# Scores by 64 rows, wider joins, and rows moved from GpSimd to ScalarE in a fused attention, FFN and scan kernel

## The reference, cut to what matters

```
x = x + attention(norm(x))      # 16 heads of 8; key k for query q if
                                #   k<=q and (k>q-32  or  (q-k)%64==0)
x = x + ffn(norm(x))            # 128 -> 512 -> 512 -> 128, weights of +1 and -1, relu
y = norm(x)
x = x + (y + scan_block(y))     # see below
x = x + ffn(norm(x))            # the same weights again

scan_block(y):                  # in the reference _mamba_block, x is y
  u, z  = split(norm(y)*g + b @ W_in)       # 2 x 256 channels
  u     = silu(causal_conv4(u))
  dt_lo, B, C = split(u @ W_xp)             # 8, 16, 16
  dt    = softplus(dt_lo @ W_dt + b_dt)     # 256 channels
  h[t]  = exp(dt*A) * h[t-1] + dt*u*B       # 256 channels x 16 states
  return res_scale * ((sum_n h*C + u*D) * silu(z)) @ W_out
```

## Time and profile before

| | |
|---|---|
| median of 3 runs | 811.17 us (809.6 to 815.29) |
| the profiled execution | 811.52 us |
| its span, first to last instruction | 809.7 us |
| mean granted TensorE clock | 0.989 of full speed |
| PE busy | 721.4 us (89%) |
| DVE busy | 695.3 us (86%) |
| POOL busy | 664.2 us (82%) |
| ACT busy | 594.8 us (73%) |
| DMA queue, 153.5 MB | 71.4% of 16 engines' span |

### The profile page before, as it was taken

One profiled execution on the slowest core, in us unless ns is written; L12 is line 12 of the kernel. 1 busy time (PEld: TensorE's weight loads), 2 busy tenths in 40 slices (PEclk: granted clock), 3 DMA queues, 4 the chain that ended last, 5 costly groups with the idle time before them and its releaser, 6 DMA issues. The chain is left out here.

```text
span 809.7 us, 22189 instructions
## 1 busy us (share of the span) xinstructions
PE 721.4 (89%) x7840; PEld 430.6 (53%) x7840; DVE 695.3 (86%) x1187; ACT 594.8 (73%) x1161; POOL 664.2 (82%) x824
## 2 busy tenths in 40 slices
PE   5999988998789999998999999899896889897887
PEld 3765655644455447545555456355452356453566
DVE  6977229999999989999889999999998989799983
ACT  5776698797788989887689978868667744764533
POOL 5143437998899989989999799899998999999961
PEclk9999999999999999999999999999999999998999
DMA  5000019888799668877777889889797899898950
GB/s 200 3 3 2 2 54 269 226 231 229 206 225 237 159 173 238 230 177 200 198 213 197 225 233 243 232 230 244 207 253 199 252 259 240 215 266 235 264 158 27
DMA packets 84177, 154.94 MB, mean 191 GB/s; under 512 B 9433, under 2 KB 10082, under 8 KB 84066
## 3 DMA queue, kind: packets, MB, share of 16 engines
q1 hardware_dynamic: 84066, 153.51, 71.4%
HBM read 142.46 MB, written 11.01 MB: 190 GB/s over the span
## 5 line engine op out<-in xcount | busy, mean ns | idle before, releaser
L1779 POOL TENSOR_TENSOR d<-d,cr 128x1024 f32<-128x1024 f32 x128 | 300.0, 2354 | 13.8 <-DVE d L1279 4.1
L1578 ACT ACTIVATE ps<-dt,An 128x512 f32<-128x512 f32 x256 | 173.7, 690 | 71.9 <-DVE d L1279 60.5
L1279 DVE TENSOR_TENSOR_SCAN d<-ps,hl,d 128x512 f32<-128x512 f32 x128 | 157.0, 1262 | 3.7 <-ACT ps L1578 3.3
L1279 DVE TENSOR_TENSOR_SCAN d<-ps,d 128x512 f32<-128x512 f32 x128 | 149.6, 1202 | 7.2 <-ACT ps L1578 6.5
L1267 DVE TENSOR_TENSOR d<-ps,d 128x512 f32<-128x512 f32 x184 | 118.5, 671 | 7.1 <-DMA d<-dud 7.1
L891 PE MATMUL ps<-h,w 128*128 128x512 f16 (+1 forms) x512 | 114.3, 373 | 3.5 <-DVE h L1224 2.8
L1766 POOL TENSOR_TENSOR d<-d,br 128x512 f32<-128x512 f32 x72 | 91.5, 1277 | 4.3 <-DMA d<-dud 4.3
L891 PEld LDWEIGHTS ps<-h,w 128*128 128x128 f16 x512 | 46.8, 98 | 70.9 <-DVE h L1224 12.8
L966 PE MATMUL ps<-d,cst 128*32 128x512 f32 x512 | 69.3, 614 | 10.6 <-POOL d L1779 6.4
L1434 ACT COPY pt<-ps 128x512 f32<-128x512 f32 x96 | 53.8, 589 | 13.9 <-PE ps L825 10.6
L825 PE MATMUL ps<-cst,sx 128*128 128x128 f32 x384 | 56.3, 281 | 8.0 <-ACT sx L1427 3.5
(11 more groups left out here) (182 smaller groups left out, 1457.1 us busy)
## 6 DMA issues: line engine op xcount, KB each, us to landing
dt<-dtd SPq DMA_DIRECT2D x256, 256.0 KB, 5.3
d<-dud SPq DMA_DIRECT2D x256, 256.0 KB, 4.8
dtd<-sR SPq DMA_DIRECT2D x16, 256.0 KB, 4.4
dud<-sE SPq DMA_DIRECT2D x16, 256.0 KB, 3.8
X<-in_x SPq DMA_DIRECT2D x8, 256.0 KB, 6.3
br<-bcd SPq DMA_DIRECT2D x8, 256.0 KB
cr<-bcd SPq DMA_DIRECT2D x8, 256.0 KB
out<-X SPq DMA_DIRECT2D x3, 512.0 KB, 5.8
```

The costliest lines, as they stand in the source:

```text
L1279: eng.tensor_tensor_scan(d, banks[u % NG][:, :], d, hl[:, r:r + 1] if m % 2 else 0.0, ALU.mult, ALU.add).then_inc(v_sc, 1)
L1578: eng.activation(banks[u % NG][:, :], DT[:, u % NT, :], ACT.Exp, scale=An[:, g:g + 1]).then_inc(s_da, 1)
L1779: eng.tensor_tensor(d, d, CR[m % 2][:, :].unsqueeze(1).to_broadcast((128, n, 512)), ALU.mult).then_inc(p_cm, n)
```

## The change

1. **Scores by 64 rows.** A unit, far or near, now holds half of the heads: 8 windows x 8 heads for far, 4 windows x 8 heads for near. `KD` has two blocks of heads per 64 partitions in place of four; a factor `rmask` blanks the other 32 partitions. Every unit pair has its masks and products on the two halves of TensorE's rows.
2. **Joins.** Two a batch instead of four, each for 512 rows and all heads; one `FR` and one `JW` in place of two.
3. **Rows by ScalarE.** Apart from one half of batch 0's attention and the first two FFN passes (`SHARED`), ScalarE normalises all rows, and a new step `mxu_s` updates X. `mno_s` takes over the two waits that `mln_p` had.
4. **Places.** All due times are new, and so is `WARM`: 33 places with 176 products, 26 of them before the first scan, instead of 28 with 152. The FFN order and the split of the drives stay.

```diff
-UNITS = [(kind, g, kk) for kind, g in GROUPS for kk in range(2 if kind else 4)]
-def near(u):
-    return (u - 8) % 4 // 2, u % 2
+UNITS = [(kind, g, kk, c) for kind, g in GROUPS for kk in range(1 if kind else 2) for c in range(2)]
...
+SHARED = FFN_ORDER[:2]
+def shared_to(i):
+    return min(i, len(SHARED))
...
-JOINS = [(b, g) for b in range(NB) for g in range(4)]
+JOINS = [(b, h) for b in range(NB) for h in range(2)]
...
-        KD = sb("KD", [128, 4, PAD + T])
+        KD = sb("KD", [128, 2, PAD + T])
...
-        ZN = [sb(f"zn{i}", [128, 8, 4, 9]) for i in range(2)]
-        MN = [sb(f"mn{i}", [128, 8, 4]) for i in range(2)]
+        ZF = [sb(f"zf{i}", [128, 8, 2, 16]) for i in range(3)]
+        ZN = [sb(f"zn{i}", [128, 16, 4, 9]) for i in range(2)]
+        MN = [sb(f"mn{i}", [128, 16, 4]) for i in range(2)]
         FC = sb("fc", [128, 2, T])
-        FR = [sb(f"fr{i}", [128, 2, 8, 2, 16]) for i in range(2)]
-        JW = [sb(f"jw{i}", [128, 4, 32]) for i in range(2)]
-        JT = sb("jt", [128, 256])
+        FR = sb("fr", [128, 16, 4, 16])
+        JW = sb("jw", [128, 4, 64])
+        JT = sb("jt", [128, 512])
...
-            def scores(b, u, mk):
-                U = NU * b + u
-                bank = bank_of["sc", b, u] = turn((s_exp, U + 1) if u in SHIFTED_T else (v_sub, shifted(b, u, "v") + 1))
-                eng.matmul(bank[:, :], e4[:, :], mk, start=True, stop=False, skip_group_check=True)
-                return bank
             def asc_t(b, u):
-                kind, g, kk = UNITS[u]
+                kind, g, kk, _ = UNITS[u]
                 U, gi = NU * b + u, group_of(u)
+                nw = 8 if kind else 4
                 if U == 0:
                     eng.wait_ge(v_set, V_SEL)
-                if kind:
-                    bank = scores(b, u, masks[:, 256:288].unsqueeze(1).to_broadcast((128, 16, 32)))
-                else:
-                    kk, _ = near(u)
-                    if g == kk == 0:
-                        mk = masks[:, 0:256].unsqueeze(1).to_broadcast((128, 2, 256))
+                half = [slice(64 * c, 64 * c + 64) for c in range(2)]
+                two = []
+                for c in range(2):
+                    by = (s_exp, U + c + 1) if u + c in SHIFTED_T else (v_sub, shifted(b, u + c, "v") + 1)
+                    bank = bank_of["sc", b, u + c] = turn(by)
+                    if kind:
+                        mk = masks[half[c], 256:288].unsqueeze(1).to_broadcast((64, 16, 32))
+                    elif g == kk == 0:
+                        mk = masks[half[c], 0:256].unsqueeze(1).to_broadcast((64, 2, 256))
                     else:
-                        mk = masks[:, 64:192].unsqueeze(1).to_broadcast((128, 4, 128))
-                    two = [scores(b, u + c, mk) for c in range(2)]
+                        mk = masks[half[c], 64:192].unsqueeze(1).to_broadcast((64, 4, 128))
+                    eng.matmul(bank[:, :], e4[half[c], :], mk, start=True, stop=False, skip_group_check=True)
+                    two.append(bank[:, :].rearrange("p (a w k) -> p a w k", a=2, w=nw))
                 if b == 0:
                     eng.wait_ge(v_aqm, gi + 1)
                 else:
                 eng.wait_ge(s_aqk, 4 * b + 2)
                 if U == 0:
                     eng.wait_ge(v_akd, 2)
+                if b == 0 and u == 8:
+                    eng.wait_ge(p_set, 2)
+                if kind == 0 and g == 2:
+                    eng.wait_ge(p_kp, b + 1)
                 qm = QM[gi % 2]
-                if kind:
-                    bw = bank[:, :].rearrange("p (a w k) -> p a w k", a=4, w=4)
-                    Ks = KD[:, :, PAD:PAD + T].rearrange("p a (h x) -> p a h x", x=128)
-                    for k in range(4):
-                        m = 8 * g + 4 * kk + k
-                        lq = qm[:, 4 * kk + k, :, :].rearrange("p a n -> p (a n)")
-                        t = eng.matmul(bw[:, :, k, :].rearrange("p a (h x) -> p a h x", x=4), lq, Ks[:, :, :, 4 * m:4 * m + 4], start=False,
-                                       stop=(k == 3 and u not in SHIFTED_T), skip_group_check=True)
-                    t.then_inc(t_sc, 1)
-                    return
-                if g == 2:
-                    eng.wait_ge(p_kp, b + 1)
-                for k in range(4):
-                    m = 8 * g + 4 * kk + k
-                    at = 64 * (m % 16) + m // 16
+                Ks = KD[:, :, PAD:PAD + T].rearrange("p a (h x) -> p a h x", x=128)
+                for k in range(nw):
+                    wi = nw * kk + k
+                    m = 8 * g + wi
                     for c in range(2):
-                        r = slice(64 * c, 64 * c + 64)
-                        for j in range(2):
-                            o = slice(64 * j, 64 * j + 64)
-                            lq = qm[r, 4 * kk + k, 2 * j:2 * j + 2, :].rearrange("p a n -> p (a n)")
-                            dst = two[c][o, :].rearrange("p (a w k) -> p a w k", a=2, w=4)[:, :, k, :]
-                            t = eng.matmul(dst, lq, KD[r, 2 * c:2 * c + 2, at:at + 127:2], start=False,
-                                           stop=(k == 3 and u + c not in SHIFTED_T), skip_group_check=True)
-                        if k == 3:
+                        end = k == nw - 1 and u + c not in SHIFTED_T
+                        if kind:
+                            for j in half:
+                                lq = qm[half[c], wi, j.start // 32:j.stop // 32, :].rearrange("p a n -> p (a n)")
+                                t = eng.matmul(two[c][j, :, k, :].rearrange("p a (h x) -> p a h x", x=4), lq, Ks[half[c], :, :, 4 * m:4 * m + 4],
+                                               start=False, stop=end, skip_group_check=True)
+                        else:
+                            at = 64 * (m % 16) + m // 16
+                            lq = qm[half[c], wi, :, :].rearrange("p a n -> p (a n)")
+                            t = eng.matmul(two[c][:, :, k, :], lq, KD[half[c], :, at:at + 127:2], start=False, stop=end, skip_group_check=True)
+                        if k == nw - 1:
                             t.then_inc(t_sc, 1)
...
             def akd_v(b, h):
                 if h == 0:
-                    eng.wait_ge(p_set, 3)
                     eng.wait_ge(t_aqk, 1)
-                    for a in range(4):
-                        t = eng.tensor_copy(KD[32 * a:32 * a + 32, a, PAD:PAD + T:2], bank_of["aqk", b, 0, 1][32 * a:32 * a + 32, :])
+                    for a in range(2):
+                        t = eng.tensor_scalar(KD[:, a, PAD:PAD + T:2], bank_of["aqk", b, 0, 1][:, :], rmask[:, a:a + 1], None, ALU.mult)
...
-            def aback_v(b, g):
-                J = 4 * b + g
-                if J >= 2:
-                    eng.wait_ge(p_jw, 5 * (J - 1))
+                eng.transpose(FC[:, c, 256 * g:256 * g + 256].rearrange("p (w q) -> p w q", w=8),
+                              ZF[(8 * b + u) % 3][:, :, :, :].rearrange("p w a n -> p w (a n)")).then_inc(v_far, 1)
+            def aback_v(b, h):
+                J = 2 * b + h
+                if J:
+                    eng.wait_ge(p_jw, 4 * J)
                 eng.wait_ge(v_far, 8 * b + 8)
-                far = FC[:, :, :].rearrange("p c (m h x i) -> p c i h m x", h=8, x=2, i=2)
+                far = FC[:, :, :].rearrange("p c (o m k x i) -> p c i k o m x", o=2, k=8, x=2, i=2)
                 for c in range(2):
-                    eng.transpose(FR[g % 2][:, c, :, :, :].rearrange("p (j o) a n -> p j (o a n)", o=2).rearrange("p j (m x) -> p j m x", x=2),
-                                  far[:, c, g // 2, 4 * (g % 2):4 * (g % 2) + 4, :, :]).then_inc(v_back, 1)
-            def jrec_v(b, g):
-                J = 4 * b + g
+                    eng.transpose(FR[:, :, 2 * c:2 * c + 2, :].rearrange("p (j o) a n -> p j o (a n)", o=2).rearrange("p j o (m x) -> p j o m x", x=2),
+                                  far[:, c, h, :, :, :, :]).then_inc(v_back, 1)
...
-            def jmix_p(b, g):
-                J = 4 * b + g
-                fr, zn, _, jw = parts(g)
+            def jmix_p(b, h):
+                J = 2 * b + h
+                fr, zn, _, jw = parts(h)
                 eng.wait_ge(v_jr, J + 1)
-                for i in (1, 0):
-                    eng.tensor_tensor(jw[i], jw[i], jw[2], ALU.mult).then_inc(p_jw, 1)
+                eng.tensor_tensor(JW[:, 0:2, :], JW[:, 0:2, :], jw[2].unsqueeze(1).to_broadcast((128, 2, 64)), ALU.mult).then_inc(p_jw, 1)
+                eng.wait_ge(p_jw, 4 * J + 1)
                 for i, x in ((1, zn), (0, fr)):
-                    eng.wait_ge(p_jw, 5 * J + 2 - i)
-                    for c in range(2):
-                        t = eng.tensor_tensor(x[:, c, :, :, 0:8], x[:, c, :, :, 0:8], jw[i][:, c, :, :].unsqueeze(3).to_broadcast((128, 8, 2, 8)), ALU.mult)
-                    t.then_inc(p_jw, 1)
-                eng.wait_ge(p_jw, 5 * J + 4)
-                for c in range(2):
```

(59 more changed lines are left out.)

397 lines of the change are left out of this document (194 added, 203 removed), and 320 rows, old and new, of tables (PLACES, WARM).

## The result

| | before | after |
|---|---|---|
| median of the runs (4 each) | 810.5 us (809.6 to 815.29) | 799.91 us (798.72 to 800.94) |
| ratio, 95% interval | | 0.9845 [0.9805, 0.9885] |
| the profiled execution, its span | 811.52, 809.7 | 800.71, 798.9 |
| mean granted clock | 0.989 | 0.981 |

On a second chip the kernel after took 799.2 us against 814.5, a ratio of 0.9794 [0.9739, 0.9849]: faster by 1.5 to 2%.

What follows compares the result with a forecast made beforehand. VectorE and GpSimd, both 93% busy between the scans, were taken as the bound. Span 809.7 - 1 + (3 - 3 - 3 - 8) + 1.5 = 799.2, so 801 us timed; range 788 to 820, the forecast's own 793 to 805.

Steps and rivals of the forecast that it cites:

- VectorE's idle time: Between first and last scan: a sign of the forecast, to fall from 47.5 us to under 40.
- GpSimd's relief, -8: Between the scans: less GpSimd work shortens VectorE's waits, 5 us for drive loads and 3 for direct waits.
- ScalarE's blocks, +3: Between the scans: 31 longer ScalarE row blocks can delay decays; 3 taken at about 1 us, ends 0 and +31.
- rival C: Between scans: ScalarE's four-row blocks hold up the decays, making the kernel slower, 818 to 824 us; chance 0.14.
- VectorE's work, -3: Between the scans: half as many, twice as wide transposes and additions save VectorE 3 us (-8 to +1).
- TensorE's scores, -3: Between the scans: cheaper score pairs save TensorE 10 us in three batches and halve VectorE's 5.4 us of score waits.
- the 1.7 that I set as the mark: TensorE's far pair: under 1.7 us would show the forecast right, over 2.5 the rival of failed packing.
- the term of 3 us that the rule would have added: TensorE's scores: if changing the tiling mode drains the array, the sum would be about 3 us higher.
- Ahead of the first scan, -1: Before the first scan: cheaper scores against a bigger join, ScalarE's rows and 26 fillers, 1 us saved (+3 to -4).
- The tail, +1.5: After the last scan: rows in sequence on ScalarE and a third layer moved there cost 1.5 us (0.5 to 4).
- My mark for the last stretch: Last 64 loads with their scans: taking longer than 62 us would show the forecast wrong.

Runs made afterwards that it cites:

- rows_only: Kernel before, in its old order, with only the rows and the X update moved to ScalarE alone: 831.16 us, ratio 1.0188.
- rows_shared: Kernel after with the rows shared by halves with GpSimd again and the X update by GpSimd: 816.62 us, ratio 1.0013.
- pool_ballast: Kernel after with unneeded 128 x 128 tiles written by GpSimd where rows and X update stood before: 807.3 us, ratio 0.9897.
- xu_split: Kernel after with ScalarE's X update cut into four one-row steps between decays: 800.76 us, ratio 0.9838.
- pe_ballast2: Kernel after with filler products on TensorE ahead of both masks of a pair, three far and one near: 829.3 us, ratio 1.0155.
- after_again: Kernel after, unchanged, timed once more as the standard for runs beside it: 799.2 us.
- The ballasts: Kernel after with unneeded work added on one engine: GpSimd 807.3 us, ScalarE 811.62, VectorE 806.58, TensorE 841.19 and 829.3.
- no_fill_head: Kernel after without the 26 filler products ahead of the first scan: 823.09 us, ratio 1.0112.

## Why the prediction was right, and where its steps were not

The time was forecast at 801 and came at 799.9, the span at 799.2 and came at 798.9. That the span hit within 0.3 us is luck. By VectorE's work and waits the terms missed by +4.1 (scores), +1.1 (ahead of the first scan), -1.3 (decays), -1.7 (tail) and -0.6 (work), 1.8 us of small waits that no term had went away besides, and these cancel. Beside the second chip's 814.5 the gain is 15 us, not 11. VectorE's idle time, which was to be under 40 us, is 40.4. Step by step:

- **GpSimd's relief, -8: the size came, the way to it is not what I wrote.** VectorE's wait for loads was to go from 7.1 to 2.1 us and went to 1.9. Busy time between the scans was forecast at 564 and is 555, a join at 6.3 us and is 6.0 (36.1 in six). The strided 512-column form takes 1.07 to 1.20 us, so the plain form's 1.28 was the right neighbour. (One of the ten instructions has 128 columns, as in my sum, not two, as in my text.) The other 3 us were to come from direct waits for GpSimd, and these gave nothing: softplus fell from 2.7 to 2.0 and the join's two from 1.9 to 0.3, but the scans now wait 2.5 for GpSimd's drives. What made up for it was ScalarE's Exp, 7.5 to 4.4, where I expected nothing. Nor do the runs bear out that GpSimd's relief is behind either of the two waits that fell. With GpSimd relieved in the old order (rows_only) VectorE waits 8.6 us for loads and 7.4 for Exp, as before; with GpSimd 32 us busier in the new order (rows_shared) 1.3 and 3.8, and with the ballast on it (pool_ballast) 1.1 and 4.0. Both waits went with the new order and what else changed, not with GpSimd's load. What loading GpSimd does cost comes elsewhere: as waits for its drives and for decays.
- **ScalarE's blocks, +3: held as a sum, on a condition that I did not state.** Busy time was forecast at 527 and is 517; the wait for decays was to stay under 13 and is 11.5, a cost of 1.7. But the same blocks in the old order doubled that wait and cost 16 us (rows_only). So rival C is no matter of the blocks alone but of the order too, and xu_split shows that in the new order the blocks of the X update, 7 of the 31, cost nothing.
- **VectorE's work, -3: -3.6.** Transposes of 512 columns take 0.68 and 0.70 us, as taken from the 0.692 of the earlier trace rows.
- **TensorE's scores, -3: this term failed, it is +1.1.** The low end of the instruction prices was right: 1.41 and 1.24 us a pair, a far pair under the 1.7 that I set as the mark. But VectorE's waits for scores, of which I took half, rose from 5.4 to 6.5. The 12 us that TensorE lost between the scans show in no wait that names the scores. By the rule in the Trainium skill, TensorEngine Tiling (Array Packing), Key Properties, changing the tiling mode drains the array; the timeline shows no gap at the changes, and the term of 3 us that the rule would have added is not there.
- **Ahead of the first scan, -1: +0.1.** I priced the 26 fillers at nothing, as work in TensorE's idle places. 115.75 us of TensorE less 9.83 of fillers is 9.6 less than the 115.52 before, and the first scan came no sooner. Without the fillers it comes 11 us later, but that is not their price: 6.3 of it are two gaps, of which pe_ballast2 has the like with more fillers, and some 2 the half clock behind the long one. What the missing fillers cost by themselves ahead of the scan is at most some 3 us, 1.6 by 107 us and 1.3 at 120 (an estimate from the timelines of the two kernels). They hold the clock up there, and I had them at nothing; where the 9.6 us of TensorE went that should have brought the first scan forward is not shown.
- **The tail, +1.5: -0.2.** The rows in a row on ScalarE cost nothing that shows, nor did the third layer that moved behind the last scan.
- **My mark for the last stretch was missed.** I wrote that the forecast would be wrong if the last 32 scans took more than 62 us. They took 67.7 (66.1 in after_again), and the forecast held only since the 576 us before gave 16.4. ScalarE's timeline there shows how it went:

```profile
733.48 0.60 ACT L1477 ACTIVATE h<-ps 128x512 f32<-128x512 f32 x1 [2.37 <-PE ps L877]
736.90 0.60 ACT L1477 ACTIVATE h<-ps 128x512 f32<-128x512 f32 x1 [2.82 <-PE ps L877]
737.39 0.69 ACT L1574 ACTIVATE ps<-dt,An 128x512 f32<-128x512 f32 x1
```

```profile
738.11 1.28 DVE L1264 TENSOR_TENSOR_SCAN d<-ps,hl,d 128x512 f32<-128x512 f32 x1 [2.42 <-ACT ps L1574]
```

An FFN copy stands ahead of the decay on ScalarE's queue and waits 2.4 and 2.8 us for a layer on TensorE, whose clock is 0.87 in this stretch (0.94 before) and 0.50 from 730.3 to 737.0; the scan behind the decay waits 2.42. It is VectorE's longest wait for a decay between the scans. The kernel before has the half clock for as long (0.50 from 734.0 to 740.6) and VectorE waits 0.7 us for decays in its whole last stretch, where the kernel after's waits 4.9. So the clock by itself does not explain the loss; that the copy's place ahead of the decay does is argued from this timeline, and no run moved it.

**The ballasts' prices do not add up to the gain.** At 0.41 us for GpSimd, 0.53 for ScalarE, 0.44 for VectorE and 0.6 for TensorE, the changes in busy time (-51.4, +21.7, -3.6, -11.7) would give -21 + 11.5 - 1.6 - 7 = -18 us, where 10.7 came. And by the same prices rows_shared (+32.4 on GpSimd, -26.2 on ScalarE) would be even with the kernel after, where it is 17.4 slower. In these queues it counts where a step stands, more than how long an engine works. How the 10.7 divide among the parts is therefore not shown. What is shown: rows on ScalarE lose 16 us in the old order (rows_only), and the new order gives nothing with half of the rows and the X update on GpSimd (rows_shared). The 64-row scores and the wider joins were never run without the rest, so what they give, and whether the new order would pay by itself, is open.

## What to carry to other kernels

Where every queue is laid out for given durations, an engine at 80% (ScalarE here) may have no free time: each of the four passed on 0.4 to 0.6 of what was added to it. Move work together with the order, and don't judge a part by a trial in the old order: it can lose what the whole gains. When a wait gets shorter as forecast, check in a run that changes the supposed cause alone whether it was the cause. Before calling filler products on TensorE idle work, look at the granted clock in the stretch behind them, in windows short enough to tell whether the clock fell before TensorE stood or after.

## What the runs showed of the hardware

- Without the 26 filler products ahead of the first scan (9.8 us) the granted clock was 0.50 at 120 to 122 us, where it was 1.00 with them, and the kernel lost 24 us, of which the gaps below are a part. Without all 176 the mean granted clock of the run was 0.932 for 0.981, and the kernel lost 32 us.
- While TensorE stood in the long gap (no_fill_head from 130.3 to 135.6, pe_ballast2 from 134.9 to 139.8) the granted clock fell from 1.00 to 0.50.
- Four kernels have a gap of 3.3 to 5.6 us on TensorE inside a run of products, with nothing that releases it, each with a 16 KB packet of an instruction queue recorded in it while the data queue held the DMA engines at over 100% (share 1.04 to 1.06). TensorE resumes 2.6 to 2.9 us after the packet starts, and the gap before it comes 125 matmul instructions earlier in the three kernels that have one. In the kernel after, two such packets (127.3 and 136.3 us) fall with no gap beside them. That the gap is the load of instructions is argued from this; what decides between gap and none stays open.
- Two masks of 64 rows ran in the time of one of 128 (0.39 and 0.38 us), 16 instructions on halves in the time of 32 on quarters (1.07 and 1.14).
